# One stage in place of three: constants, first layer norm and the tables of q, k and v of a graph network on one NeuronCore

## The chip, the cores and the metric

The kernel runs on one core of one Trainium2 chip. The metric is device time in microseconds (us) of that core; lower is better. The core's engines are TensorE (PE in the rows; PEld is its weight load), VectorE (DVE), ScalarE (ACT), GpSimd (POOL) and SyncE (SP), which here issues DMAs. They run side by side and wait for each other through semaphores.

## The reference

The program is a two-layer graph network over N = 3125 nodes with 256 features and E = 50000 edges, sorted by destination. What the change touches is its very start: a layer norm of the nodes, three linear maps of it, and for each edge the product of its destination's key with its source's query.

```python
def _layernorm(x, axis=-1, eps=1e-05):
    m = jnp.mean(x, axis=axis, keepdims=True)
    v = jnp.var(x, axis=axis, keepdims=True)
    return (x - m) / jnp.sqrt(v + eps)
...
h = _layernorm(x)
q, k, v = h @ Wq.T + bq, h @ Wk.T + bk, h @ Wv.T + bv     # 3125 x 256 each
score[e, head] = sum over the head's 64 features of k[dst[e]] * q[src[e]]
```

These lines of the maps are told in short; in the program, softmax over each node's edges, sums of v, a global attention, experts, a graph convolution, a spline layer, an attention in the Poincare ball and a last layer of experts follow. All of them stay as they are.

## The kernel before, in words

Nodes lie in NT = 25 tiles of 128 rows (padded to 3200). Work is cut into stages; a stage has one instruction stream for each engine, and between two stages all engines meet at a barrier. A stage's `Chain` c(...) makes VectorE wait for each of its own instructions before the next.

The kernel begins with three stages, one after the other:

- `constants` (L266 on) loads the destinations of the edges and all of x, and builds what the later loops read: the identity `m.ident`, bf16 copies of the destinations (`m.lines`, `m.pick`, by GpSimd), and the list of steps. A step is a pair of 128-edge tiles and a window of 128 node slots. VectorE finds the ends of every run of edges (L338 to L353), TensorE sums counts (L384 to L386), VectorE compares 4992 step numbers with two columns (L363), TensorE turns that into words by 78 one-column products (L390), and the words go out to memory and come back as one row, `m.steps`.
- `layer_norm` (L143 on) does statistics of all 25 tiles (L158), seven small operations over all of them (L134 to L140), a square root on ScalarE (L188), a reciprocal, and 25 scalings (L169). Each tile is turned by two TensorE transposes (L180) and copied out by two ScalarE copies (L194) into `m.xT`.
- `node_tables` (L200 on) loads weights and biases, then for every tile makes three products of two 128x256 matmuls each (L234) in a ring of five PSUM banks; VectorE adds the bias of each (L246) and SP stores it to memory (L221): q and v side by side in `table_qv`, k in `table_k`.

Then `edge_scores` begins. Its SP stream first loads all of k back (L486) to the 25 first of 49 slots of `k`; ScalarE and VectorE copy it, shifted by half a tile, to the other 24 (L558, L802). Only then may TensorE's key products begin (L633). The loop goes by rounds of RING = 8 steps. For each step ScalarE copies two columns of source numbers (L519), GpSimd gathers 2 x 128 rows of `table_qv` by an indirect DMA each (L613) into one of eight buffers, TensorE spreads the edges' numbers (L625), VectorE makes a one-hot of them (L807), TensorE fetches the keys by it (L633), VectorE multiplies with the gathered q (L814) and reduces (L821), and SP stores the gathered v by edge (L503). GpSimd's gather of step s+8 waits for VectorE's multiplication of step s. Beside the steps TensorE and ScalarE do the work of a global attention: in the first five rounds (FIRST) a projection of two 128x320 matmuls every second step, in the next five (HIDE) a hidden layer and exponentials, then other pieces (SECOND, THIRD).

The order within each engine is the order in which the code is written; nothing schedules it.

Of the kernel before, what the change touches and what calls it, by code (L numbers as in the profile page):

```python
# [8 lines left out]
F32 = mybir.dt.float32  # L9
# [7 lines left out]
P = 128  # L17
# [108 lines left out]
def tiles_in(tt):  # L126

    return [tt * U + u for u in range(U)]


# [12 lines left out]
def layer_norm(nc, name, src, rows, cols, ident, banks, spread=None):  # L143


    with Stage(nc, name) as st:
# [3 lines left out]
        var_ready, std_ready, rows_ready = st.sem("var"), st.sem("std"), st.sem("rows")  # L150
        transposed, copied, own = st.sem("transposed"), st.sem("copied"), st.sem("own")
        with nc.Block() as block:
            @block.vector
            def _(dve):
                c = Chain(dve, own)
                with dve.Fori(0, TU) as tt:
                    for t in tiles_in(tt):
                        nc.vector.bn_stats(stats[:, bass.ds(t, 1), :], src[:, bass.ds(t, 1), :]).then_inc(own, 1)  # L158
                c.n = NT
                dve.wait_ge(own, NT)  # L160
                mean_and_variance(nc, c, stats, mv, rstd)
                if spread is not None:
                    c(nc.vector.tensor_copy(spread[:], mv[:, :, 1]))
                dve.sem_inc(var_ready, 1)
                dve.wait_ge(std_ready, 1)
                c(nc.vector.reciprocal(rstd[:], rstd[:]))
                with dve.Fori(0, TU) as tt:
                    for t in tiles_in(tt):
                        nc.vector.tensor_scalar(rows[:, bass.ds(t, 1), :], src[:, bass.ds(t, 1), :],  # L169
                                                mv[:, bass.ds(t, 1), 0], rstd[:, bass.ds(t, 1)],  # L170
                                                ALU.subtract, ALU.mult).then_inc(rows_ready, 1)

            @block.tensor
            def _(pe):
                for tt in range(TU):
                    for u in range(U):
                        pe.wait_ge(rows_ready, tt * U + u + 1)
# [17 lines left out]


def node_tables(nc, name, cols, weights, biases, tables, banks, spare):

    n = len(tables)
    with Stage(nc, name) as st:  # L200
        w = st.sb("w", [P, n, FT, F])
# [2679 lines left out]
```

## Time and profile before

| | us |
|---|---|
| three runs | 3152.86, 3153.89, 3155.55 (median 3153.89) |
| profiled execution, its own time | 3153.17 |
| its span, first to last instruction | 3151.5 |
| mean granted TensorE clock | 0.933 |

Over the whole span PE is busy 84%, DVE 63%, ACT 43%, POOL 34%. The shares are means over some dozen stages with different limits, and the change lies in the first 4% of the span and in what follows on it. So what has to be read is the timeline of the first 160 us and the loop behind it. All times in the rows count from the first instruction; they belong to the one profiled execution.

### The profile page before, as it was taken

What the parts mean: (1) busy time and instruction counts of PE and PEld (TensorE: products, weight loads), DVE (VectorE), ACT (ScalarE), POOL (GpSimd) and SP (SyncE); (2) the same over time, 40 slices, a digit from 0 to 9 for tenths busy, and PEclk for the clock granted to TensorE, in tenths of its full rate; (3) what the DMA queues carried; (4) which work ended last, traced back from release to release, by engine and by line L of the source; (5) the groups of instructions that cost most, each with busy time, mean ns of one, the idle gap of its engine ahead of it and who ended that gap; (6) DMA issues with size and microseconds to landing.
All of it is one profiled execution on the core that took longest, in us unless ns stands there. A gap on an engine that the chain in (4) does not pass through costs nothing. (4 is left out here: it accounts for less than half of the span.)

```text
span 3151.5 us, 54706 instructions
## 1 busy us (share of the span) xinstructions
PE 2657.6 (84%) x12020; PEld 2080.1 (66%) x12021; DVE 1989.4 (63%) x3891; ACT 1355.5 (43%) x2868; POOL 1074.7 (34%) x1184
## 2 busy tenths in 40 slices
PE   4677788737994899999997999999959996869798
PEld 3545555424552677777775888888848874647587
DVE  5386677877888444435214666666689986965411
ACT  1013332207882333333332444444459966855222
POOL 1276677742112000000003666666600006820043
PEclk9898899968997899999998999999979998989899
DMA  3698899956775000000004777777711114033253
GB/s 103 223 303 282 273 309 309 313 144 197 219 219 177 1 1 9 1 9 9 1 9 160 213 214 215 215 212 214 215 29 42 38 47 152 1 137 118 75 179 130
DMA packets 246940, 450.34 MB, mean 143 GB/s; under 512 B 29767, under 2 KB 142351, under 8 KB 245418
## 3 DMA queue, kind: packets, MB, share of 16 engines
q1 hardware_dynamic: 189868, 268.45, 27.2%
q0 software_dynamic: 56960, 180.47, 18.3%
q8 instruction: 62, 1.02, 0.1%
q14 instruction: 50, 0.41, 0.0%
HBM read 353.83 MB, written 95.96 MB: 143 GB/s over the span
## 5 line engine op out<-in xcount | busy, mean ns | idle before, releaser
L1826 PE MATMUL bank<-conv_w,conv_eT 128*128 128x256 f32 x2352 | 541.2, 380 | 4.2 <-DMA conv_eT<-in_edges 4.2
L1826 PEld LDWEIGHTS bank<-conv_w,conv_eT 128*128 128x128 f32 x2352 | 434.1, 190 | 56.2 <-DMA conv_eT<-in_edges 5.0
L1758 POOL DMA_INDIRECT conv_h<-table_h,conv_ix x392 | 389.0, 992 | 211.9 <-issue 113.1
L613 POOL DMA_INDIRECT x<-table_qv,scores_ix x300 | 283.8, 946 | 235.0 <-ACT scores_ix L519 157.0
L1523 ACT ACTIVATE area<-bank,nodes_bi,nodes_sc 128x320 f32<-128x320 f32 x320 | 197.5, 617 | 378.6 <-PE bank L1440 378.6
L1671 DVE SCALAR_TENSOR_TENSOR x<-bank,nodes_w,x 128x256 f32<-128x256 f32 x200 | 96.6, 484 | 324.4 <-PE bank L1449 324.3
L1782 DVE TENSOR_TENSOR conv_msg<-bank,conv_h 128x512 f32<-128x512 f32 x196 | 135.5, 692 | 193.8 <-PE bank L1826 193.8
L1290 PE MATMUL bank<-attend_pv,x 128*128 128x260 f32 x800 | 221.1, 404 | 30.4 <-POOL attend_pv L1221 26.4
L633 PE MATMUL bank<-sums,area 128*128 x800 | 233.0, 420 | 11.3 <-issue 6.3
L519 ACT ACTIVATE scores_ix<-src 128x2 int32 x200 | 40.5, 203 | 408.1 <-DVE area L814 327.7
L1290 PEld LDWEIGHTS bank<-attend_pv,x 128*128 128x128 f32 x800 | 137.2, 191 | 114.1 <-issue 66.2
L1725 ACT ACTIVATE conv_ix<-src 128x2 int32 x196 | 39.8, 203 | 366.6 <-DVE conv_msg L1782 344.2
L633 PEld LDWEIGHTS bank<-sums,area 128*128 128x128 f32 x800 | 154.3, 208 | 55.1 <-issue 31.1
L1181 ACT ACTIVATE x<-area,scores 128x128 f32 x400 | 157.3, 398 | 26.1 <-PE bank L1290 9.0
L1411 POOL MEMSET sums<- 128x1300 f32 x5 | 5.9, 1181 | 441.5 <-DVEq L1630 441.5
L1918 PE MATMUL bank<-xT,sums 128*128 128x256 f32 x700 | 155.2, 379 | 0.0
L625 PE MATMUL bank<-lines,pick 128*128 x200 | 58.4, 292 | 102.9 <-DVE area L807 70.4
L1918 PEld LDWEIGHTS bank<-xT,sums 128*128 128x128 f32 x700 | 133.0, 190 | 18.1
L814 DVE TENSOR_TENSOR area<-x,bank 128x512 f32<-128x512 f32 x150 | 103.0, 686 | 66.2 <-PE bank L633 56.2
L1238 DVE TENSOR_TENSOR attend_pv<-x,probs 128x512 f32<-128x512 f32 x198 | 135.9, 686 | 13.2 <-issue 13.2
L1839 PE MATMUL bank<-conv_coarse,conv_hot 128*128 128x256 f32 x392 | 137.9, 374 | 1.1 <-DVE conv_fine L1787 1.1
L821 DVE TENSOR_REDUCE scores_dot<-area 128x8 f32<-128x512 f32 x200 | 135.1, 675 | 0.1
(473 smaller groups left out, 5775.8 us busy)
## 6 DMA issues: line engine op xcount, KB each, us to landing
conv_eT<-in_edges SPq DMA_DIRECT2D x196, 384.0 KB
x<-edge_v SPq DMA_DIRECT2D x200, 256.0 KB, 3.0
edge_v<-x SPq DMA_DIRECT2D x150, 256.0 KB, 4.6
hidden_rows<-top_wide SPq DMA_DIRECT2D x25, 512.0 KB, 3.5
projected<-spline_hst SPq DMA_DIRECT2D x10, 960.0 KB, 4.4
ball_hT<-projected SPq DMA_DIRECT2D x5, 1920.0 KB, 19.1
top_wd<-in_top_wd SPq DMA_DIRECT2D x8, 1024.0 KB
table_qv<-sums SPq DMA_DIRECT2D x50, 128.0 KB, 1.7
```

Of the source, the lines that this page charges most:

```text
L613: nc.gpsimd.indirect_dma_start(out=qv(u)[:, g - u * G, :], out_offset=None, in_=m.d_qv, in_offset=bass.IndirectOffsetOnAxis(ap=ix[:, g:g + ...
L633: mm = nc.tensor.matmul(banks[u % UN][:, g * F:(g + 1) * F], hotT[:, u % UN, g * P:(g + 1) * P], k[:, bass.ds(t, 1), :].rearrange("p t f - ...
L821: nc.vector.tensor_reduce(dot[:, u % 2], qk[:, u % 2].rearrange("p (g h d) -> p g h d", g=G, h=HEADS), AX.X, ALU.add).then_inc(reduced, 1)
L1181: nc.scalar.activation(hot[:, u, g * P:(g + 1) * P], m.ids[:, bass.ds(t, 1)].rearrange("p t n -> p (t n)"), ACT.Abs, bias=minus[:, bass.ds ...
L1238: nc.vector.tensor_tensor(pv[:, u, :, 0:F].rearrange("p g (h d) -> p g h d", h=HEADS), v[:, u].rearrange("p g (h d) -> p g h d", h=HEADS), ...
L1290: mm = nc.tensor.matmul(banks[u][:, 0:WIDE], hot[:, u, g * P:(g + 1) * P], pv[:, u, g], start=g == 0, stop=g == G - 1)
L1523: nc.scalar.activation((h1, h2)[layer][:, o, hf * CW:(hf + 1) * CW], banks[n % HIDS][:, 0:CW], ACT.Relu, scale=sc[:, layer, e, o:o + 1], b ...
L1758: nc.gpsimd.indirect_dma_start(out=h[:, u, g, :], out_offset=None, in_=m.d_h, in_offset=bass.IndirectOffsetOnAxis(ap=ix[:, u * G + g:u * G ...
L1782: nc.vector.tensor_tensor(msg[:, u % 2], wide(u), h[:, u], ALU.mult).then_inc(messaged, 1)
L1826: mm = nc.tensor.matmul(banks[u][:, g * F:(g + 1) * F], eT[:, u, g, c], w[:, c], start=False, stop=c == EC - 1, skip_group_check=True)
L1839: nc.tensor.matmul(acc(u), hot[:, u, g], coarse[:, u, g], start=g == 0, stop=False)
L1918: mm = nc.tensor.matmul(out, spl[:, t % SETS, k, f * P:(f + 1) * P], ws[:, f, k], start=False, stop=f == FT - 1 and k == KS - 1)
```

## The change

The three stages become one, `front`. It loads x in five chunks of five tiles, and goes by chunks: `moments(n)` (statistics and the seven small operations on one chunk), `normal(n)` (reciprocal and five scalings), and for each tile two transposes, one copy, and the products of q, k and v. The step list's parts are put between the tiles, at tiles numbered by COUNT = 3 and LIST = 9. q and k use three PSUM banks, v two of its own: ScalarE writes v's bias into the bank ahead of the product (`seed`), the product is accumulated on it, and ScalarE copies it out (`keep_v`). VectorE adds the biases of q and k only; k's result goes straight to its slot in `keys`, which is `edge_scores`' `k`. q and v leave in one store. The table of k and its load are gone. The scratch for `number`, `lines_i`, `dst_i` and others moves to other buffers.

```diff
+def front(nc, a, m, banks):
...
+                def rows_of_x(n):
+                    sp.dma_start(m.x[:, tiles(n)], a["x"][n * U * P:(n + 1) * U * P].rearrange("(t p) f -> p t f", p=P)).then_inc(x_in[n], 16)
+                rows_of_x(0)
+                sp.dma_start(rows_i.rearrange("r g e -> r (g e)"), a["dst_scan"]).then_inc(pairs, 16)
+                for j, n in enumerate("qkv"):
+                    sp.dma_start(w[:, j], a[f"gnn_w{n}"]).then_inc(loaded, 16)
+                    sp.dma_start(b[:, j], a[f"gnn_b{n}"]).then_inc(loaded, 16)
+                rows_of_x(1)
                 for half in range(2):
                     sp.dma_start(lines_i[half * LINES:(half + 1) * LINES], a["dst_lines"]).then_inc(ends_loaded, 16)
+                for n in range(2, TU):
+                    rows_of_x(n)
...
+                for t in range(NT):
+                    sp.wait_ge(biased, 2 * t + 1)
+                    sp.wait_ge(kept_v, t + 1)
+                    sp.dma_start(m.d_qv[t * P:(t + 1) * P, :], qv[:, t % U]).then_inc(stored[t % U], 16)
...
+            @whole.tensor
+            def _(pe):
...
+                def turn(t):
+                    pe.wait_ge(rows_ready, t + 1)
+                    if t >= 2:
+                        pe.wait_ge(copied, t - 1)
+                    for f in range(FT):
+                        tr = nc.tensor.transpose(bank_x(t)[:, f * P:(f + 1) * P], m.rows[:, t, f * P:(f + 1) * P], m.ident[:])
+                    tr.then_inc(turned, 1)
+
+                def products(t):
+                    pe.wait_ge(copied, t + 1)
+                    for j in range(2):
+                        i = 2 * t + j
+                        if i >= 3:
+                            pe.wait_ge(biased, i - 2)
+                        for f in range(FT):
+                            mm = nc.tensor.matmul(bank(i), m.xT[:, f, t * P:(t + 1) * P], w[:, j, f], start=f == 0, stop=f == FT - 1)
+                        mm.then_inc(product, 1)
+                    pe.wait_ge(seeded, t + 1)
+                    for f in range(FT):
+                        mm = nc.tensor.matmul(bank_v(t), m.xT[:, f, t * P:(t + 1) * P], w[:, 2, f], start=False, stop=f == FT - 1,
+                                              skip_group_check=True)
+                    mm.then_inc(made_v, 1)
+                turn(0)
+                pe.wait_ge(loaded, 32 * KINDS)
+                for t in range(NT):
+                    if t + 1 < NT:
+                        turn(t + 1)
+                    products(t)
...
+            @whole.scalar
...
+                for t in range(NT):
+                    if t + 1 < NT:
+                        columns(t + 1)
+                    if t % U == 1 and t // U + 1 < TU:
+                        root(t // U + 1)
+                    keep_v(t)
+                    if t + 2 < NT:
+                        act.wait_ge(kept_v, t + 1)
+                        seed(t + 2)
...
+                moments(0)
                 dve.wait_ge(pairs, 16)
+                c(nc.vector.tensor_copy(rows_f, rows_i))
+                normal(0)
+                c(nc.vector.tensor_reduce(ends[:, 0], rows_f, AX.X, ALU.min))
...
+                dve.sem_inc(counted, 1)
...
+                for t in range(NT):
+                    n = t // U
+                    if t % U == 0 and n + 1 < TU:
+                        moments(n + 1)
+                    bias(t)
+                    if t % U == 2 and n + 1 < TU:
+                        normal(n + 1)
+                    if t == COUNT:
+                        first_steps()
+                    if t == COUNT + 1:
+                        compare(seen[:, 0:1], early)
+                    if t == COUNT + 3:
+                        compare(begin[:], late)
+                    if t == COUNT + 2:
+                        rounds()
...
 def edge_scores(nc, a, m, banks):
...
-                sp.dma_start(k[:, 0:NT], m.d_k.rearrange("(t p) f -> p t f", p=P)).then_inc(k_loaded, 16)
...
-                act.wait_ge(k_loaded, 16)
                 nc.scalar.activation(k[0:P // 2, NT:SLOTS], k[0:P // 2, 1:NT], ACT.Copy).then_inc(k_spread, 1)
```

Of the order, first TensorE at its start. In the program before, everything of the step list stands ahead of a barrier, then the transposes, then, behind another barrier, the products (`const_`, `norm_` and `qkv_` are the three stages' names):

```order
L384 MATMUL bank<-const_sums,const_before 99x1 [waits const_tables,const_made]
L385 MATMUL bank<-const_sums,const_next_to 99x1
L386 MATMUL bank<-const_one,const_sums 1x1
L390 MATMUL bank<-const_change,rows 128x1 [waits const_tables]
L390 MATMUL bank<-const_change,rows 128x1 x77
L287 UNCONDITIONAL_BRANCH
L173 UNCONDITIONAL_BRANCH [waits barrier_Pool_Activation_PE_DVE_SP_release]
L180 MATMUL bank<-ident,rows 128x128 [waits norm0_copied,norm0_rows]
```

In the changed one this is TensorE from the end of tile 2 to the transposes of tile 5 (`front_` is the stage; L290 are q and k, L294 is v):

```order
L305 MATMUL bank<-front_sums,front_before 99x1 [waits front_counted]
L306 MATMUL bank<-front_sums,front_next_to 99x1
L307 MATMUL bank<-front_one,front_sums 1x1
L280 MATMUL bank<-ident,rows 128x128 [waits front_copied,front_rows_ready]
L280 MATMUL bank<-ident,rows 128x128
L290 MATMUL bank<-front_w,xT 128x256 [waits front_biased,front_copied]
L290 MATMUL bank<-front_w,xT 128x256
L290 MATMUL bank<-front_w,xT 128x256 [waits front_biased]
L290 MATMUL bank<-front_w,xT 128x256
L294 MATMUL bank<-front_w,xT 128x256 [waits front_seeded]
L294 MATMUL bank<-front_w,xT 128x256
L280 MATMUL bank<-ident,rows 128x128 [waits front_copied,front_rows_ready]
```

The transposes and the products of a tile now alternate, and each q or k product waits for a bias addition of VectorE, three products back. The second place is VectorE around the first comparison. Before:

```order
L359 TENSOR_TENSOR const_begin<-const_seen,const_count 99x1 [waits const_own]
L360 TENSOR_TENSOR const_change<-const_slot,const_seen 99x1 [waits const_own]
L363 TENSOR_SCALAR rows<-sums,const_seen 99x4992 [waits const_made,const_own]
L363 TENSOR_SCALAR rows<-sums,const_begin 99x4992 [waits const_own]
L366 CAST dst<-const_dst_i 128x396 [waits const_own,const_edges]
```

Now, from the additions of tile 4 to the first addition of tile 5:

```order
L373 TENSOR_TENSOR front_qv<-bank,front_b 128x256 [waits front_product,front_own]
L375 TENSOR_TENSOR sums<-bank,front_b 128x256 [waits front_product]
L407 TENSOR_SCALAR area<-area,front_seen 99x4992 [waits front_numbered]
L357 BN_STATS front_stats<-x 128x6 [waits front_x_in2]
L357 BN_STATS front_stats<-x 128x6 x4
L129 TENSOR_TENSOR front_mean_var<-front_stats 128x5 [waits front_own]
L130 TENSOR_TENSOR front_rstd<-front_stats 128x5 [waits front_own]
L131 TENSOR_SCALAR front_mean_var<-front_mean_var 128x5 [waits front_own]
...
L135 TENSOR_SCALAR front_mean_var<-front_mean_var 128x5 [waits front_own]
L373 TENSOR_TENSOR front_qv<-bank,front_b 128x256 [waits front_own,front_stored0,front_product]
```

The comparison and a chunk's moments stand one behind the other between two pairs of additions for which TensorE waits.

## Rows read from the trace of the kernel before

**Rows 1.** Stages of the start: length, busy time of each engine, granted clock, DMA.

```profile
...
0.00:27.00 27.00, 3.16 (x84) 3.00 (x85) 18.27 (x35) 0.02 (x1) 11.64 (x20) 1.00 0.55 167
27.00:51.00 24.00, 8.89 (x50) 6.72 (x50) 18.66 (x59) 10.63 (x52) 0.00 (x0) 1.00 0.00 1
...
57.00:125.00 68.00, 66.96 (x300) 58.31 (x300) 31.83 (x75) 0.00 (x0) 0.00 (x0) 0.97 0.41 139
...
```

**Rows 2.** Timeline of the first 15 us: start, length, engine, line, operation, wait.

```profile
...
2.27 4.47 POOL L316 IOTA sums<- 99x4992 f32 x1
...
3.69 3.35 DVE L338 CAST const_rows_f<-const_rows_i 99x512 f32<-99x512 int32 x1 [3.57 <-DMA const_rows_i<-in_dst_scan]
...
8.92 0.99 DVE L343 TENSOR_SCALAR const_tile_i<-const_ends_i 99x2 int32<-99x2 int32 x1
...
9.97 2.36 POOL L329 TENSOR_TENSOR lines<-xT,lines 64x1152 bf16<-64x1152 f32 x1
10.14 2.21 DVE L345 CAST const_tile<-const_tile_i 99x2 f32<-99x2 int32 x1
...
13.86 0.16 DVE L353 SCALAR_TENSOR_TENSOR const_sums<-const_slot,const_count 99x1 f32<-99x1 f32 x1
...
```

**Rows 3.** DMA issues up to 140 us: count, size, median us to landing.

```profile
...
x<-in_x SPq DMA_DIRECT2D x1, 3200.0 KB, 14.2
...
```

**Rows 4.** Groups of instructions, 0 to 50 us: count, busy us, mean ns, idle.

```profile
...
L180 PE MATMUL bank<-ident,rows 128*128 128x128 f32 x50 | 8.9, 324 | 16.9 <-DVE rows L169 16.9
...
L158 DVE BATCH_NORM_STATS2 norm_stats<-x x25 | 8.4, 413 | 4.7 <-PEq L287 4.3 <-issue 0.3
L169 DVE TENSOR_SCALAR rows<-x,norm_mean_var,norm_rstd x25 | 8.4, 407 | 0.4 <-DVE norm_rstd L166 0.4
...
L363 DVE TENSOR_SCALAR rows<-sums,const_seen 99x4992 bf16<-99x4992 f32 x1 | 2.8, 2819 | 0.0
...
L390 PE MATMUL bank<-const_change,rows 99*128 99x1 bf16 x78 | 2.2, 165 | 6.5 <-DVEq L364 6.5
...
```

**Rows 5.** Groups of instructions, 51 to 125 us.

```profile
...
L234 PE MATMUL bank<-qkv_w,xT 128*128 128x256 f32 x300 | 67.0, 387 | 7.5 <-DMA qkv_b<-in_gnn_bv 7.5
...
L246 DVE TENSOR_TENSOR sums<-bank,qkv_b 128x256 f32<-128x256 f32 x75 | 31.8, 424 | 44.0 <-PE bank L234 44.0
```

**Rows 6.** Timeline of TensorE, 55 to 64 us.

```profile
...
57.14 7.17 PE L234 MATMUL bank<-qkv_w,xT 128*128 128x256 f32 x23 [7.46 <-DMA qkv_b<-in_gnn_bv]
```

**Rows 7.** Timeline from 124 us on: the end of the tables, the start of edge_scores.

```profile
...
124.14 0.42 DVE L246 TENSOR_TENSOR sums<-bank,qkv_b 128x256 f32<-128x256 f32 x1 [0.44 <-PE bank L234]
...
128.62 0.41 SPq L486 DMA_DIRECT2D sums<-table_k  x1
...
130.28 1.16 POOL L613 DMA_INDIRECT x<-table_qv,scores_ix  x1 [117.48 <-ACT scores_ix L519]
...
147.50 5.32 ACT L558 ACTIVATE sums<-sums 64x6144 f32<-64x6144 f32 x1 [14.90 <-DMA sums<-table_k]
147.50 3.39 DVE L802 COPY sums<-sums 64x6144 f32<-64x6144 f32 x1 [15.78 <-DMA sums<-table_k]
148.02 3.69 POOL L613 DMA_INDIRECT area<-table_qv,scores_ix  x1 [0.31 <-issue]
...
155.59 0.69 DVE L814 TENSOR_TENSOR area<-x,bank 128x512 f32<-128x512 f32 x1 [3.79 <-PE bank L633]
...
157.52 0.94 POOL L613 DMA_INDIRECT x<-table_qv,scores_ix  x1 [4.57 <-ACT scores_ix L519]
...
```

**Rows 8.** Group of ScalarE's copy out of PSUM, 125 to 175 us.

```profile
...
L567 ACT ACTIVATE rows<-bank 128x320 f32 x4 | 1.7, 437 | 0.4 <-PE bank L640 0.4
...
```

**Rows 9.** VectorE's timeline at the end of edge_scores' first five rounds.

```profile
...
246.87 0.69 DVE L814 TENSOR_TENSOR area<-area,bank 128x512 f32<-128x512 f32 x1
...
```

**Rows 10.** The gathers' line, 125 to 250 us: time to landing.

```profile
...
DMA to landing us min/median/max: 4.4/5.3/8.2
```

**Rows 11.** The gathers' line alone: POOL busy and count in a stretch.

```profile
...
175.00:250.00 75.00, 56.71 (x60) 1.00 0.97 314
...
```

More of the change, by code:

```diff
@@ new lines, in front @@
+        x_in = [st.sem(f"x_in{n}") for n in range(TU)]
+        filled, made, numbered, halved, named = (st.sem(x) for x in ("filled", "made", "numbered", "halved", "named"))
+        own, counted, added, begun, listed, worded, steps_kept = (
+            st.sem(x) for x in ("own", "counted", "added", "begun", "listed", "worded", "steps_kept"))
+        var_ready, std_ready, rows_ready, turned, copied = (
+            st.sem(x) for x in ("var_ready", "std_ready", "rows_ready", "turned", "copied"))
@@ new lines, in front, with tiles, bank, bank_v @@
+        opened, seeded, product, biased, made_v, kept_v = (
+            st.sem(x) for x in ("opened", "seeded", "product", "biased", "made_v", "kept_v"))
+        stored = [st.sem(f"stored{u}") for u in range(U)]
+        STORE_WORDS, COUNT, LIST = 17, 3, 9
+        def tiles(n):
+            return slice(n * U, (n + 1) * U)
+        def bank(i):
+            return banks[i % 3][:, 0:F]
+        def bank_v(t):
+            return banks[3 + t % 2][:, 0:F]
+        def bank_x(t):
+            return banks[5 + t % 2][:, 0:F]
@@ L359, in _ @@
-                c(nc.vector.tensor_tensor(begin[:], seen[:, 0:1], count[:, 0:1], ALU.add))
-                c(nc.vector.tensor_tensor(change[:, 0:1], slot[:, 0:1], seen[:, 1:2], ALU.subtract))
-                dve.wait_ge(made, 5)
-                for k, first in enumerate((seen[:, 0:1], begin[:])):
-                    c(nc.vector.tensor_scalar(begun[:, k], number, first, None, ALU.is_ge))
-                dve.sem_inc(tables, 1)
-                dve.wait_ge(edges, 16)
-                c(nc.vector.tensor_copy(m.dst[:], dst_i[:]))
@@ new lines, in compare, with rounds @@
+                def compare(first, to):
+                    dve.wait_ge(numbered, 1)
+                    nc.vector.tensor_scalar(to, number, first, None, ALU.is_ge).then_inc(begun, 1)
+                def rounds():
+                    for k, many in enumerate((UN, RING)):
+                        for j in range(2):
+                            c(nc.vector.tensor_scalar(m.rounds[:, 2 * k + j:2 * k + j + 1], banks[7][0:1, TOTAL_AT:TOTAL_AT + 1],
+                                                      float(many - 1 - j * many), float((FEWEST[many] - j) * many), ALU.add, ALU.max))
+                        c(nc.vector.tensor_scalar(m.rounds[:, 2 * k:2 * k + 2], m.rounds[:, 2 * k:2 * k + 2], many.bit_length() - 1, None, ALU.arith_shift_right))
@@ L395, in step_at @@
+                c(nc.vector.tensor_copy(m.twice[:], mv[:, :, 1]))
 def step_at(eng, m, s):
```

296 lines of the change are left out of this document (125 added, 171 removed).

## The prediction

> **What bounds the kernel now.** I read the stretches of the start first, then the timeline inside them, then the first rounds of the loop behind, since a gain at the start is kept only if nothing there gives it back.
>
> The start falls into four pieces, and in each another engine works [rows 1]. To 27 us VectorE is busy 18.3 us and TensorE 3.2. From 27 to 51 us VectorE works 18.7 us and TensorE 8.9. From 57 to 125 us TensorE is busy 67.0 of 68 us and VectorE 31.8. So TensorE's products are the longest piece, and some 57 us in which TensorE hardly works lie ahead of them. The products take 67.0 us for 300 records [rows 5]; the first 23 ran in 7.17 us [rows 6], at half clock in part. Twelve records make a tile. The other 277 take 59.8 us, 0.216 us each, 2.59 us a tile.
>
> Behind it, edge_scores begins at 128.62. Its k load holds VectorE's and ScalarE's copies until 147.50, the first score comes at 155.59, and GpSimd, which had begun to gather at 130.28, stands idle 4.57 us before 157.52 because all eight buffers are full [rows 7]. The k load is thus waited for, but what ends the first rounds is a second question: GpSimd issues 60 gathers in 75 us, one per 1.25 us and without a gap [rows 11], and a step needs two: 2.50 us. The fortieth score is at 246.87 [rows 9], so (246.87 - 155.59) / 39 = 2.34 us a step: TensorE and VectorE go faster than the gathers and eat up their lead. At that score some of it is left: the step's second gather was issued at 157.52 + 1.25 + 31 x 2.5 = 236.3, and with the median of 5.3 us to landing [rows 10] it was there at 241.6.
>
> **The change, part by part.** Times from here are laid out on the new program's own clock.
>
> *First chunk.* x in one piece landed 14.2 us after its issue [rows 3]; a fifth of it is 2.8 us, and the smallest load, 198 KB, took 2.8 us from 0.85 to 3.69 as well [rows 2]. I take 4.9 us for chunk 0, between 3.7 and 6. Statistics are 8.4 / 25 = 0.336 us a tile [rows 4], 1.7 a chunk. A small dependent operation costs about 0.19 us: twelve of them, L343 to L353, took 5.1 us, less the two that stood for GpSimd (0.8 and 2.0 over their own length) [rows 2]. Seven are 1.4 us, so moments(n) costs 3.1. The first tensor_scalar of moments(0) meets GpSimd's IOTA, 4.47 us, which held up L338 from 3.69 to its end at about 7 before [rows 2]; it now starts one 0.6 us memset later. moments(0) ends near 8.4, the root and the cast near 9, normal(0) (0.3 + 5 x 0.336 = 2.0) at 11.
>
> *Counting, and the second moments, ahead of the first addition.* Two reductions 1.4, fourteen small operations 2.7, and GpSimd's three copies of the lines, which now land after x0, the weights and x1 and so fall again into this chain: the two waits seen before (2.8 us) up to three (4.2). That is 19 us, 17.8 without the third wait. moments(1) stands next: 22.1. Only then bias(0). TensorE has begun by about 11, has made q, k, v of tile 0 and q of tile 1, and stops for a bank until 22.5.
>
> *From there on.* k and v of tile 1: 1.7. Twenty-three tiles at 2.59 for the products plus two transposes. These took 8.9 / 50 = 0.18 each [rows 4], paced by VectorE, which bounds them from above at 0.36 a tile; from below, half the columns of one product record, 0.108 each, 0.22 a tile. I take 0.30: 23 x 2.89 = 66.5. The 78 products of the list: 2.2 [rows 4]. After a pause of some 5 us the clock is low as at 57 us: 7.17 - 23 x 0.216 = 2.2 lost [rows 6]. ScalarE is no bound: three passes over 256 columns a tile, each no more than the 0.44 of a 128x320 one [rows 8], 1.3 of 2.9 us; they hide behind the products, and at over 2.9 would be the pace. VectorE needs 0.85 a tile for two additions [rows 5], and with moments, normals and comparisons some 48 of 75 us.
>
> *The ring of three banks.* From the end of q(t) TensorE has k, v, the next transposes and the next q before it, 2.9 us, until it needs q(t)'s bank back; VectorE is free 1.5 us ahead of q(t)'s end and needs 0.5 for the addition. So work of up to 3.9 us put ahead of an addition costs nothing. One moments(n) (3.1) or comparison (2.8 [rows 4]) fits. At tile 4 to 5 they stand together: 5.9, a stall of 2.1; the second comparison and normal(2) follow before VectorE has caught up: 0.7 more. Taken: 2.8. Bounds: 0, and 24 if nothing hid (three more moments 9.3, four normals 8, comparisons and small ones 9, less 2.8).
>
> So TensorE ends at 22.5 + 1.7 + 66.5 + 2.2 + 2.2 + 2.8 = 97.9. Before, from the last addition's release at 124.14 to edge_scores' first instruction at 128.62 it took 4.5 us [rows 7]: copy, store, landing, barrier. The same again gives 102.4 instead of 128.62: 26.2 us gained. The stores, one of 256 KB a tile instead of three of 128, are in the shadow of the products as before.
>
> *edge_scores.* Counted from its start. Before, the copies began at 18.9 and the first score stood at 27.0. Now ScalarE does its eight source copies (to 4.0) and then copies for 5.3 [rows 7]; the first score comes 14.8 earlier, at 12.2. GpSimd begins at 1.7 as before and is held up once by VectorE's 3.39 us copy, as its 3.69 us gather shows [rows 7]; that merely comes earlier. Without the 4.3 us that the full ring cost (4.57 less the usual 0.3), the second gather of step 8 starts at 157.52 + 1.25 - 4.27 - 128.62 = 25.9 and that of step 39 at 25.9 + 31 x 2.5 = 103.4; it lands at 108.7. The score of step 39 was at 118.3, and 14.8 earlier would be 103.5. The gathers now end last: 118.3 - 108.7 = 9.6 us gained, between 6.7 and 10.5 by the extremes of landing, 8.2 and 4.4 [rows 10]. Behind it comes other work per round, in which the ring was full again before, so I carry the 9.6 to the end.
>
> **Sum.** 26.2 + 9.6 = 35.8 from the profiled execution's 3153.17 is 3117.4; the median of the runs is 0.7 above that execution, so 3118.
>
> **The rivals.**
> (a) *The gathers swallow the k load's share.* If GpSimd's chain sets the pace not only of these rounds but of all of edge_scores, only its 4.3 us of idleness are gained: 26.2 + 4.3, 3123. For it: 1.25 us without a gap [rows 11]. Against: the fortieth score before did not wait for them.
> (b) *VectorE as the bound of the new stage.* If the three banks hide nothing, 24 us instead of 2.8: 3139. For it: VectorE alone is busy 37 us in the two early stages [rows 1], and all of this now goes between additions. Against: the slack of 3.9 us.
> (c) *Slower: TensorE stays at half clock in front.* It now mixes transposes and waits for three other engines into what was a closed run of products. At half clock a tile costs 2.59 us more, 23 tiles 60 us: 3178. It turns a gain into a loss from 35.8 / 2.59, 14 tiles, on. Against it: the transposes alone stood at granted clock 1.00 between 27 and 51 us [rows 1], the products at 0.97 with their cold start; gaps above 5 us are not foreseen after the first.
> The Trainium skill speaks for (c): TensorE: Matmul & The Clock Gate, section Part 4: PE-mode transpose, says that a transpose does not count as busy for the clock. By that rule the two transposes of each tile would be idle time, a tenth of it; the trace before, with 1.00 over a stretch of transposes alone, does not show it, though that stretch began in quiet and is weak evidence.
> (d) *Front starts earlier or its order stalls less:* no lock waits and no stall, 4.2 + 2.8 less: 3111. This and the like lie in the forecast's own range.
>
> **How the numbers follow.** The forecast's case, 3108 to 3128: 0.72. (a) alone lies in it; with a start worse by 5 to 8 us it leads to 3132: 0.08. (b) or half of it, 3130 to 3142: 0.12. (c) 0.02. Better than 3108, with the full 14.8 us of k and a start without locks (3118 - 5.2 - 7): 0.06. The range 3106 to 3132 leaves out about 2 in 10. A difference under 0.2% (6 us) can't be told from none in this kernel. Faster by more than that: all but (c) and an unknown of the same size, 0.96; within 0.01; slower 0.03.
>
> **What would show it.** Right: TensorE pauses from about 17 to 22 us and once near tiles 4 to 6; the products' pace between is 2.8 to 3.0 us a tile; edge_scores' first instruction at 98 to 107 us; the first score 12 us later; in the first five rounds VectorE's multiplication waits for the gathers' landing, not for TensorE, and GpSimd has no idle time but 0.3 us a piece. Wrong: TensorE waiting for VectorE at every chunk (b), a granted clock under 0.9 in front (c), rounds of HIDE or later that are longer than before, or scores 40 and 200 whose distances from edge_scores' start have shrunk by other than some 10 us.

## The result, and the profile after

The changed kernel takes 3103.07 us, the median of 4 runs (3099.56 to 3106.83), against 3154.47 us for the kernel before on the same chip. The ratio on record is 0.9844, with a 95% interval from 0.9828 to 0.9861 (the two medians by themselves would give 0.9837). Two later batches on other chips came to 0.9848 and 0.9858. The forecast was 3118 us, with a range from 3106 to 3132: the sign was right, the gain was larger than forecast, and the median lies 2.9 us below the range. The three ratios average 0.9850, a gain of 47.3 us; by that figure the time would be near 3107 us, just inside the range, so a miss of the range by this little is in part the scatter of one batch. The gain itself is a third larger than the 35.8 us forecast, and that is no scatter. The profiled execution has a span of 3097.9 us and a time of its own of 3099.56 us.

The stretches of the new start, one line each (length, busy time of each engine, granted clock, DMA share, GB/s), in place of those of [rows 1]:

```profile
0.00:22.00 22.00, 9.48 (x26) 6.62 (x27) 15.07 (x49) 4.25 (x11) 11.57 (x20) 1.00 0.91 257
24.00:94.00 70.00, 67.82 (x404) 58.93 (x403) 41.67 (x124) 24.50 (x70) 0.00 (x0) 0.98 0.23 85
```

One stretch of TensorE's work is left where there were two of VectorE's ahead of one of TensorE's. From 24 to 94 us TensorE is busy 67.8 of 70 us. The timeline of the changed kernel shows how it gets there (start, length, engine, line, operation, and the wait in brackets):

```profile
2.55 4.47 POOL L251 IOTA area<- 99x4992 f32 x1
5.48 1.73 DVE L357 BATCH_NORM_STATS2 front_stats<-x 128x6 f32<-128x256 f32 x5 [5.36 <-DMA x<-in_x]
7.25 0.17 DVE L129 TENSOR_TENSOR front_mean_var<-front_stats 128x5 f32<-128x5 f32 x1
...
9.47 1.71 DVE L367 TENSOR_SCALAR rows<-x,front_mean_var,front_rstd 128x256 f32<-128x256 f32 x5
...
11.10 3.78 PE L290 MATMUL bank<-front_w,xT 128*128 128x256 f32 x8
...
15.25 1.73 DVE L357 BATCH_NORM_STATS2 front_stats<-x 128x6 f32<-128x256 f32 x5
15.77 1.14 POOL L259 CAST sums<-sums 128x1152 f32<-128x1152 int32 x1 [8.50 <-DMA sums<-in_dst_lines]
16.97 1.15 POOL L261 CAST lines<-sums 128x1152 bf16<-128x1152 f32 x1
17.02 1.12 DVE L129 TENSOR_TENSOR front_mean_var<-front_stats 128x5 f32<-128x5 f32 x1
18.17 0.17 DVE L130 TENSOR_TENSOR front_rstd<-front_stats 128x5 f32<-128x5 f32 x1
18.20 2.37 POOL L263 TENSOR_TENSOR lines<-sums,lines 64x1152 bf16<-64x1152 f32 x1
18.37 2.22 DVE L131 TENSOR_SCALAR front_mean_var<-front_mean_var 128x5 f32<-128x5 f32 x1
...
21.61 0.42 DVE L373 TENSOR_TENSOR front_qv<-bank,front_b 128x256 f32<-128x256 f32 x1
22.09 1.50 PE L290 MATMUL bank<-front_w,xT 128*128 128x256 f32 x4 [4.70 <-DVE front_qv L373]
...
40.82 1.13 PE L290 MATMUL bank<-front_w,xT 128*128 128x256 f32 x4 [2.18 <-DVE front_qv L373]
...
64.31 0.38 PE L280 MATMUL bank<-ident,rows 128*128 128x128 f32 x2
64.53 1.89 PE L290 MATMUL bank<-front_w,xT 128*128 128x256 f32 x8
...
67.13 0.38 PE L280 MATMUL bank<-ident,rows 128*128 128x128 f32 x2
...
94.15 1.03 PE L294 MATMUL bank<-front_w,xT 128*128 128x256 f32 x4
```

TensorE pauses twice: for 4.70 us, until VectorE has made the first addition of tile 0 and a bank is free, and for 2.18 us at tile 5. Two operations of five columns that take 0.17 us elsewhere take 1.12 and 2.22 us and end 0.02 us after GpSimd's operations of 16.97 and 18.20 do; these are the waits that [rows 2] showed in the counting, now in moments(1). A tile takes 67.13 - 64.31 = 2.82 us.

The start of edge_scores, in place of [rows 7], and VectorE's multiplication of the fortieth step, in place of [rows 9]:

```profile
99.20 0.34 SPq L542 DMA_DIRECT2D vec<-in_mix_wk  x1
...
100.78 1.16 POOL L667 DMA_INDIRECT x<-table_qv,scores_ix  x1 [79.75 <-ACT scores_ix L574]
...
102.25 3.54 POOL L667 DMA_INDIRECT x<-table_qv,scores_ix  x1 [0.30 <-ACT scores_ix L574]
102.31 3.36 DVE L855 COPY sums<-sums 64x6144 f32<-64x6144 f32 x1
...
102.76 5.31 ACT L612 ACTIVATE sums<-sums 64x6144 f32<-64x6144 f32 x1
...
110.83 0.69 DVE L867 TENSOR_TENSOR area<-x,bank 128x512 f32<-128x512 f32 x1 [4.26 <-PE bank L687]
...
208.01 0.69 DVE L867 TENSOR_TENSOR area<-area,bank 128x512 f32<-128x512 f32 x1 [0.57 <-DMA area<-table_qv,scores_ix]
```

edge_scores starts at 99.20 instead of 128.62, the first score comes 11.6 us after that instead of 27.0, and the fortieth at 108.8 instead of 118.3. What the fortieth waits for is the gather's landing, as forecast; nine of the forty multiplications waited for a landing, 4.6 us in all, and GpSimd was never idle for more than 0.3 us between gathers.

In the profiled executions the lead of the changed kernel is 29.4 us at the start of edge_scores and 38.9 us at the fortieth score, 3.1 more than the 35.8 of the sum. But it ends at 3151.5 - 3097.9 = 53.6 us. The other 14.7 us arise where the code is the same, so the experiments went after them above all. This table gives, from the trace of every kernel that ran, edge_scores' start; the first and fortieth score counted from it; the length of scores 41 to 81 (the HIDE rounds); the length of the attention sums (the stage behind edge_scores that sums v over each node's edges), from their first instruction to the start of TensorE's last product; what follows that; and the span. All in us.

| kernel | start | first | fortieth | HIDE | attention | behind | span |
|---|---|---|---|---|---|---|---|
| before | 128.6 | 27.0 | 118.2 | 122.1 | 248.7 | 2183.3 | 3151.5 |
| before, again | 129.6 | 27.2 | 118.9 | 121.4 | 248.8 | 2187.0 | 3159.0 |
| after | 99.2 | 11.6 | 108.8 | 117.3 | 243.6 | 2179.5 | 3097.9 |
| after, again (two) | 98.7, 99.9 | 11.6, 11.6 | 108.1, 109.2 | 117.5, 119.3 | 244.5, 244.0 | 2177.6, 2181.7 | 3098.1, 3104.4 |
| k through memory | 98.6 | 27.4 | 118.3 | 119.4 | 243.7 | 2181.1 | 3115.3 |
| after, paused | 106.3 | 11.7 | 108.2 | 117.7 | 243.7 | 2179.2 | 3108.5 |
| before, 75 memsets (two) | 131.9, 131.5 | 27.5, 27.0 | 118.2, 117.9 | 119.4, 119.8 | 244.0, 244.4 | 2181.1, 2178.8 | 3145.0, 3144.0 |
| before, 75 and 61 | 132.2 | 27.3 | 119.6 | 121.4 | 244.0 | 2178.3 | 3145.1 |
| after, reordered | 90.0 | 11.6 | 108.5 | 119.4 | 244.0 | 2181.4 | 3094.2 |
| after, comparisons later | 98.0 | 11.6 | 108.8 | 120.2 | 244.3 | 2178.6 | 3101.4 |
| after, v's bias on VectorE | 102.5 | 11.9 | 108.2 | 120.7 | 248.8 | 2179.0 | 3107.9 |
| after, 25 memsets | 99.3 | 11.6 | 108.1 | 119.2 | 249.3 | 2179.5 | 3106.0 |

### The profile page after: what moved, and what is told of

It is laid out like the page before. It is cut to its first block and busy times, and to the rows that moved or that the text cites. A ratio compares the mean times of both kernels' runs of the same rounds, so it can differ in the third digit from the quotient of the medians.

```text
span 3097.9 us, 54276 instructions
## 1 busy us (share of the span) xinstructions
PE 2648.6 (85%) x12024; PEld 2070.9 (67%) x12025; DVE 1979.6 (64%) x3898; ACT 1370.0 (44%) x2897; POOL 1067.3 (34%) x1184
## 3 DMA queue, kind: packets, MB, share of 16 engines
q1 hardware_dynamic: 179516, 261.89, 27.2%
```

## The experiments

**1. Both kernels again.** Nothing is edited.

> The changed kernel once more, nothing altered. Theory 1 (the forecast's two terms are caused by the change, the rest of the gain is not): edge_scores again starts at 99.2 us and its fortieth score comes 108.8 us later, both within 0.5 us, while the rounds behind, the attention sums and the node layers differ from the first profiled execution by some us in sum, in either direction; total 3098 to 3107. Theory 2 (everything that is gained behind the fortieth score is caused by the change as well): those stages too repeat to within 1 us in sum, total 3099 to 3101.

> The kernel before once more. Theory 1: edge_scores at 128.6 and the fortieth score 118.3 us later, within 0.5; later stages differ from the first execution by some us in sum, in either direction. Theory 2: all stages repeat within 1 us.

Measured: 3104.59 us (median of 5, ratio 0.9848, 0.983 to 0.9866), and one run of the kernel before at 3160.75, beside 3152.7 for its median in that batch. The start of edge_scores and the fortieth score repeat within 1 us, not within the 0.5 expected (128.6 and 129.6, 118.2 and 118.9; 99.2 and 98.7, 108.8 and 108.1). The attention sums too repeat within 1 us in both kernels, 248.7 and 248.8 against 243.6 and 244.5, so the 5 us between the kernels are no chance. What lies behind them differs by 3.7 us between two executions of the kernel before. So neither theory holds whole: the attention sums repeat, the rest behind the fortieth score does not.

**2. Keys through memory again.** The new front, but k goes to the table of k and is read back before the copies:

```diff
+                    sp.dma_start(m.d_k[t * P:(t + 1) * P, :], keys[:, t]).then_inc(k_kept, 16)
...
+                sp.dma_start(k[:, 0:NT], m.d_k.rearrange("(t p) f -> p t f", p=P)).then_inc(k_loaded, 16)
```

> The changed kernel with k also stored to memory, one 128 KB store a tile, and loaded back at the start of edge_scores, where the copies wait for it as before the change: only the front part of the gain is left. Theory 1: edge_scores starts at 99 to 101 us, the fortieth score 118 us after that, 9.5 us later than in the changed kernel, and the total is 9 to 11 us above it. Rival (the gathers set the pace of all of edge_scores): 4 to 5 us above it. Rival (the whole advance of the first score counts): 15 us above it.

Measured: 3114.82 us (3112.04 to 3117.04), ratio 0.9878 (0.9862 to 0.9893), 10.2 us above the changed kernel of the same batch. The first score is back at 27.4 us and the fortieth at 118.3. So the 9.6 us that the sum gave to this part are right at the fortieth score, where 9.5 are seen, and they do not get lost behind it: the two hundredth and last score comes 541.5 us after edge_scores' start here, against 525.1, 526.7 and 528.2 in the three executions of the changed kernel (the rounds between add scatter of their own). The timed 10.2 us alone would say less, since runs of the changed kernel in this batch spread over 14 us. The attention sums stay at 243.7 us: neither k's way nor its load is their cause.

**3. A pause ahead of everything.** A stage with one memset on GpSimd stands before the new front.

```diff
+        with Stage(nc, "pause") as st:
...
+                        nc.gpsimd.memset(m.rows[:], 0.0).then_inc(done, 1)
```

> The changed kernel behind a stage that holds one GpSimd memset of 25 tiles, about 6 to 7 us with its barrier; everything else is as it was, only later. If later stages depend on nothing but their own work, the total is above the changed kernel's by just the pause, 6 to 7 us. If they depend on where they stand in time (the clock's, or the phase of two engines), the total differs from that by several us and the profile names the stage.

Measured: 3113.44 us (3110.22 to 3117.33), 8.9 above the changed kernel for the 7.6 us by which edge_scores started later than in that kernel's profiled execution of the same batch (6 to 7 were expected of the pause). Time at the front reaches the end one to one within the scatter, and the attention sums stay at 243.7 us although they begin 10 us later.

**4. The place of the code.** An instruction's start is in the trace for register and branch instructions too. This is the time in ns from the start of the branch at the end of a loop's pass to the start of the next instruction on that engine; it is the same in nearly every pass of a loop:

```
                        before   again   after   again   75 memsets   75 and 61   25 on after   v on VectorE
VectorE, HIDE rounds       300     300     281     281          281         281           281            281
VectorE, attention sums    267     267     191     191          191         191           280            280
VectorE, convolution       267     267     272     272          176         176           280            280
ScalarE, HIDE rounds       155     155     155     155          155         237           155            155
ScalarE, convolution       155     155     226     226          155         226           226            155
```

The loops are word for word the same; what differs is how many instructions stand ahead of them. So memsets of one element, whose result nobody reads, were put ahead of them in the kernel before, and then in the changed one.

```diff
+                for n in range(75):
+                    nc.vector.memset(pad[:, n:n + 1], 0.0)
                 c(nc.vector.scalar_tensor_tensor(packed[:], banks[2][:, 0:COLS], 1.0, place[:], ALU.mult, ALU.add))
```

> The kernel before, with 75 one-element memsets more on VectorE in its constants stage (work that nobody waits for), so that all VectorE code behind stands 75 instructions later, about as in the changed kernel. Nothing else differs. Theory (the place of the code of a loop sets how long the jump back takes): in the attention sums VectorE's next instruction starts 267 ns after its loop's branch in both runs of the kernel before and 191 ns in all four with the new front; here it should come at 191 or at another fixed value than 267, and with it the length of the attention sums should leave 248.7 us (towards 243.7, if VectorE alone decides). Rival (something that the new front leaves in memory or in time): 267 ns and 248.7 us stay as they are.

> The kernel before, with the 75 memsets on VectorE and 61 one-element copies on ScalarE in its constants stage, so that the code of both engines stands about as late as in the changed kernel. Theory (place of code): attention sums 243.5 to 245 us instead of 248.7, of a round of eight steps 9.34 us instead of 9.55; ScalarE's branches in edge_scores' second loop and in the edge convolution take other times than 155, 237 and 155 ns. For the HIDE rounds (steps 40 to 80 of edge_scores, 122.1 and 121.4 us before, 117.3 to 117.7 after) the theory says nothing certain: if they fall to 117.5 too, it was the code's place there as well; if they stay at 122, it was the lead of the gathers. Rival (what the front leaves behind): 248.7 and 9.55 stay.

> The kernel before with the 75 memsets on VectorE, now timed. Theory (place of VectorE's code, worth 4.7 us in the attention sums of its look, less what the memsets cost at the front, where edge_scores started at 132.4 us instead of 128.6 to 129.6): the two nearly cancel in the total, ratio 0.998 to 1.000, while the attention sums stay at 244.0 and the HIDE rounds lie between 119 and 122 us. Rival (the look's 3146.7 us showed a gain of the whole kernel of 4.5 us): ratio 0.9985 or below. If the HIDE rounds come at 121 to 122 again, the 119.4 of the look was chance of the clock; at 119.4 again, it belongs to the program.

Measured: 191 ns in all three, and 244.0, 244.0 and 244.4 us of attention sums. ScalarE's 61 copies changed its own jumps but not this stage: VectorE alone decides it. Timed, the kernel with 75 memsets takes 3145.65 us against 3151.3, ratio 0.9985 (0.9974 to 0.9996), although edge_scores starts some 2.6 us later in it (131.9, 131.5 and 132.2 us in the three padded executions, counted from the load of k, against 128.6 and 129.6; the memsets stand ahead of the packing of the words). This ratio lies within the range of the theory and at the edge of the rival's, so it does not decide between them; it shows a small gain of the whole kernel. The question on the HIDE rounds stayed open as well: 119.8 us. Then the same in the other direction:

```diff
+                for n in range(25):
+                    nc.vector.memset(pad[:, n:n + 1], 0.0)
                 moments(0)
```

> The changed kernel, with 25 one-element memsets on VectorE ahead of its first moments, where it waits for x until 5.4 us. VectorE's code behind then stands where it stands in the kernel with v's bias on VectorE, in which the jump of the attention sums took 280 ns and the stage 248.8 us. Theory (place of VectorE's code): 280 ns instead of 191, attention sums 248.8 instead of 243.7 us, edge_scores' start within 0.5 us of 99, in all 4 to 6 us slower than the changed kernel by the runs on one chip. Rival (the 248.8 us there came with the other load of ScalarE and VectorE): 191 ns and 243.7 us stay, within 2 us of the changed kernel.

> The changed kernel again, beside the one with 25 memsets, as its control on the same chip: ratio 0.984 to 0.985. Its HIDE rounds (steps 40 to 80 of edge_scores) took 117.3 and 117.5 us at a granted clock of 0.86 and 0.83. If their length hangs on the clock and the clock on chance, a third execution may show 118 to 122 at 0.75 to 0.80; if it belongs to the program, 117 to 118 again.

Measured: 280 ns, attention sums of 249.3 us, edge_scores' start at 99.3, and 3109.29 us against 3104.76 on the same chip, ratios 0.9872 (0.985 to 0.9893) and 0.9858 (0.9837 to 0.988): 4.5 us more. The intervals of the two ratios overlap, so what is clear of noise is the stage in the trace and not the total. The direction and the size fit. VectorE's rows at the jump (start, length, line, the wait before) show the mechanism; first the kernel before:

```profile
903.08 0.42 DVE L1248 TENSOR_TENSOR sums<-sums,bank 128x260 f32 x1
904.05 0.69 DVE L1238 TENSOR_TENSOR attend_pv<-x,probs 128x512 f32<-128x512 f32 x1 [0.55 <-issue]
```

then the changed one:

```profile
854.23 0.43 DVE L1301 TENSOR_TENSOR sums<-sums,bank 128x260 f32 x1
855.11 0.69 DVE L1291 TENSOR_TENSOR attend_pv<-x,probs 128x512 f32<-128x512 f32 x1 [0.46 <-issue]
```

the one before with 75 memsets:

```profile
900.57 0.69 DVE L1241 TENSOR_TENSOR attend_pv<-x,probs 128x512 f32<-128x512 f32 x1 [0.46 <-issue]
```

and the changed one with 25:

```profile
852.72 0.69 DVE L1294 TENSOR_TENSOR attend_pv<-x,probs 128x512 f32<-128x512 f32 x1 [0.56 <-issue]
```

"issue" before VectorE's first multiplication of a pass holds the jump. The clock is no rival in this stage; over the attention sums of the kernel before, the changed one and the changed one with 25 memsets, the rows are

```profile
719.40:968.10 248.70, 220.67 (x799) 137.24 (x800) 214.96 (x402) 209.96 (x602) 48.49 (x201) 0.97 0.73 215
674.80:918.40 243.60, 219.42 (x800) 136.96 (x800) 214.87 (x402) 206.13 (x602) 47.16 (x201) 0.97 0.75 220
677.20:926.50 249.30, 219.85 (x800) 137.16 (x800) 216.89 (x402) 207.58 (x602) 50.81 (x201) 0.97 0.73 215
```

with the same granted clock of 0.97 and TensorE busy for the same time within 1.3 us. Over 24 passes the jump's 0.08 us make 1.9 us. A pass takes 9.55 us in the kernel before and 9.34 in the changed one, so the rest of the 0.21 comes after: most steps take 1.08 us, and in the kernel before one more step of each pass takes 1.20. Why it takes longer there was not taken apart.

A jump that moves need not cost anything. VectorE's in the convolution went from 267 to 176 ns with the 75 memsets, 4.4 us over its 48 passes, and that stage lasted 630.1 and 630.6 us without them and 630.8, 630.4 and 630.7 with them. TensorE is busy 608.7 of the 630.1 us there and VectorE 416.0.

**5. TensorE's two pauses.** moments(1) and ScalarE's root of it are moved behind the second tile's additions, and the comparisons two tiles back, with the list:

```diff
-                    if t % U == 0 and n + 1 < TU:
+                    if t % U == 0 and 0 < n and n + 1 < TU:
                         moments(n + 1)
                     bias(t)
+                    if t == 1:
+                        moments(1)
...
-                    if t == COUNT + 1:
+                    if t == COUNT + 3:
                         compare(seen[:, 0:1], early)
...
```

> The changed kernel, with two moves in the new stage: VectorE's moments of the second chunk stand behind the bias of tile 1 (ScalarE's root of it likewise behind keep_v of tile 1), and the two comparisons of the step list stand at tiles 6 and 8 instead of 4 and 6, TensorE's list two tiles later. Theory (the first bias waits behind moments(1), whose small instructions GpSimd holds up, and tile 5 waits behind a comparison): TensorE's pauses of 4.7 us at the third tile and 2.2 us at tile 5 go, edge_scores starts 5 to 7 us earlier than 98.7 to 99.2, near 93, and all of it reaches the end: near 3097 to 3099 us. Rival A (tile 4 then waits for the second chunk's moments, which are as slow behind bias(1)): the pause moves to tile 4 and 0 to 2 us are won. Rival B (GpSimd's chain of table, gathers and node numbers is what edge_scores' start really hangs on): the start does not move.

> The changed kernel with only the second move of the reordered one: the two comparisons of the step list at tiles 6 and 8, TensorE's list two tiles later; moments(1) stays ahead of bias(0). Theory: TensorE's pause of 4.7 us before the third tile's products stays, the one of 2.2 us at tile 5 goes, edge_scores starts near 97 (99.2 less 2.2), and the rest of the 9.2 us that the reordered kernel won is moments(1)'s. Rival (the two pauses share a cause, the comparison is only late because the first bias was): the pause at tile 5 moves one or two tiles on, and the start stays at 99.

Measured: 3095.87 us (3092.43 to 3099.86), ratio 0.9825 (0.9812 to 0.9839). It is the fastest kernel of the study. edge_scores starts at 90.0, 9.2 us earlier, which is more than the two pauses (6.9) and more than the 5 to 7 expected; in the time some 8 us arrive (ratio 0.9825 beside the changed kernel's 0.9850). TensorE's clock shows most of the rest. In the changed kernel the windows behind the first pause and on from it have

```profile
22.00:24.00 2.00, 1.91 (x6) 1.59 (x7) 1.07 (x4) 0.00 (x0) 0.00 (x0) 0.68 0.36 129
24.00:42.00 18.00, 15.82 (x77) 13.34 (x76) 12.15 (x39) 5.61 (x16) 0.00 (x0) 0.94 0.18 68
```

and the reordered one has, over the whole of it,

```profile
16.00:87.00 71.00, 69.61 (x414) 60.12 (x412) 46.12 (x142) 25.23 (x74) 3.85 (x4) 1.00 0.31 113
```

A granted clock of 0.68 for 2 us and 0.94 for 18 against 1.00 is some 1.7 us of the missing 2.3. With only the comparisons moved (one run, 3103.13 us) the pause at tile 5 is gone as expected, but the first pause is 5.55 us instead of 4.70, and edge_scores starts at 98.0 instead of the 97 expected. That start is worth only 1.2 us, but behind the longer first pause the clock also stayed low for longer, as this row of that kernel shows:

```profile
24.00:42.00 18.00, 18.00 (x85) 15.31 (x84) 11.21 (x41) 5.82 (x17) 0.00 (x0) 0.89 0.20 74
```

So most of the 9.2 us are moments(1)'s, and how much exactly one run does not tell.

**6. v's bias on VectorE.** The product starts afresh, and VectorE adds v's bias as it does k's.

```diff
+                    dve.wait_ge(made_v, t + 1)
+                    nc.vector.tensor_tensor(qv[:, t % U, F:2 * F], bank_v(t), b[:, 2], ALU.add).then_inc(kept_v, 1)
```

> The changed kernel, with v's bias back on VectorE: its third product starts afresh, ScalarE neither seeds nor copies v, VectorE adds 128x256 from PSUM per tile more. By the trace VectorE has 1.1 us of work per tile of 2.81 (q's and k's bias) besides moments, normal and the list, and one addition more of 0.36 us makes 1.5 to 1.6 per tile, on average below TensorE's pace: theory: tiles stay at 2.8 us, the front ends within 2 us of 99, total within 3 us of the changed kernel. Rival (ScalarE was given the bias because VectorE is full where moments, comparisons and additions meet): the stalls at tiles 2 and 5 and at each chunk grow by 0.4 to 1.5 us each, edge_scores starts 4 to 8 us later and the time is 3107 to 3111.

Measured: 3113.41 us (3109.61 to 3117.62), ratio 0.9885 (0.9869 to 0.99). edge_scores starts at 102.5, 3.3 us later: TensorE's pauses are 5.26, 3.05, 0.31 and 0.33 us instead of 4.70 and 2.18. The theory's "within 2 us of 99" failed by that, and the rival's 4 to 8 us and 3107 to 3111 us were missed a little on either side. Another 5 us of the loss have nothing to do with the bias: with 25 more additions on VectorE the jump of the attention sums took 280 ns and the stage 248.8 us, which is what the 25 memsets of experiment 4 gave by themselves.

## Why the prediction missed

*First chunk.* Forecast: x lands at 4.9, moments(0) ends near 8.4, normal(0) at 11. Measured: 5.48, 8.6, 11.2. Right. (The working counts twelve small operations from L343 to L353; they are eleven, so one costs 0.20 instead of 0.19 us, 0.2 us in all.)

*Counting, second moments, first addition.* Forecast: TensorE goes on at 22.5; measured 22.09. The lock waits were laid in the counting (4.2 us) and fell in moments(1), 0.95 + 2.05 = 3.0 us over the usual 0.17, since the lines landed late. The sum was nearly right with the waits in another place.

*From there on.* 75.4 us were forecast to TensorE's end and 73.1 measured. The transposes were sized wrongly: the lower bound of 0.22 us a tile was the truth and 0.30 was taken (23 x 0.08 = 1.8). The stall at tile 4 to 5 was forecast at 2.1 and measured at 2.18; the further 0.7 did not come. The low clock behind the first pause cost 1.7 instead of 2.2; three small products of the counting, which the sum left out, took 0.5 (28.42 to 28.90). From TensorE's end to edge_scores 4.0 us instead of 4.5. Together the front gains 29.4 instead of 26.2 us.

*edge_scores.* First score 11.6 after the start (forecast 12.2), fortieth 108.8 (forecast 108.7), and 10.2 us in the total by experiment 2 (forecast 9.6). Here the row of the gathers' line in the changed kernel alone is the counterpart of [rows 11]:

```profile
125.00:200.00 75.00, 56.73 (x61) 0.95 0.97 314
```

Rival (a) is out: had the gathers paced all of edge_scores, only 4.3 us of it would have stayed, against the 10.2 in the time and 13 to 16 at the two hundredth score in experiment 2.

*The step that failed* is the sum's last: "so I carry the 9.6 to the end", and nothing else from there on. It took the stages behind as unchanged because their code is. The prediction had named the sign itself, scores 40 and 200 nearer to edge_scores' start "by other than some 10 us": the fortieth came nearer by 9.4, the two hundredth by 15.2 (540.3 to 525.1; 543.0 in the other execution of the kernel before, 526.7 and 528.2 in the changed one's). Inserted and removed instructions ahead of them moved VectorE's code, and the attention sums alone became 4.3 to 5.1 us shorter, which is shown in both directions. The front's 3.2 us are the smaller part of the miss. The closing account: the three ratios of the changed kernel average 0.9850, 47.3 us of 3152. The kernel before gains 0.0015 x 3151 = 4.7 us by its 75 memsets (1.3 to 8.2 by the interval) while it starts edge_scores about 2.6 us later for them, so the place of the code is worth some 7.3 us, 3.9 to 10.8. That leaves 40.0 us for the change itself, 36.5 to 43.4, against 35.8 + 3.2 = 39.0 by the sum with the front as measured. This is an estimate: it takes the two programs' code as equally placed, and outside the attention sums it is not (the jumps in the table).

*What stays open* is the part of those 7.3 us outside the attention sums. The HIDE rounds took 121.4 to 122.1 us in the kernel before, 119.4 to 121.4 with memsets and 117.3 to 120.7 behind the new front. Their windows, of the kernel before,

```profile
252.40:374.60 122.20, 88.57 (x324) 63.80 (x325) 77.81 (x171) 46.67 (x95) 78.46 (x83) 0.76 0.86 267
```

of the changed kernel,

```profile
213.60:330.90 117.30, 80.64 (x324) 56.80 (x325) 77.73 (x171) 46.67 (x95) 81.70 (x87) 0.86 0.93 292
```

and of a second execution of that,

```profile
215.00:334.30 119.30, 85.60 (x324) 61.30 (x325) 77.78 (x171) 46.72 (x95) 81.57 (x87) 0.80 0.91 287
```

show nearly the same counts of instructions on TensorE, VectorE and ScalarE and another granted clock: 0.76, 0.86, 0.80. TensorE's burst for the hidden products shows it in single rows of the changed kernel:

```profile
287.19 2.94 PE L720 MATMUL bank<-wg,scores_room 128*128 128x64 f32 x20 [1.78 <-ACT scores_room L594]
...
309.30 4.43 PE L720 MATMUL bank<-wg,scores_room 128*128 128x64 f32 x20 [1.75 <-ACT scores_room L594]
```

So the HIDE rounds are mostly shorter where the clock is higher, and it varies from one execution of a program to the next. In the kernel with the comparisons moved 120.2 us stand beside a clock of 0.85, so it is not all. Whether the code's place moves the clock's chances was not settled. Behind the attention sums 2 to 9 us separate the kernels, and executions of one kernel differ there by 4. Part of that goes with the clock too; the attention in the Poincare ball, in two executions of the changed kernel, is

```profile
2546.50:2737.70 191.20, 137.36 (x600) 105.96 (x600) 156.64 (x217) 137.07 (x214) 139.83 (x83) 0.92 0.17 63
2545.60:2742.00 196.40, 142.81 (x600) 109.65 (x600) 156.77 (x217) 137.08 (x214) 139.82 (x83) 0.89 0.17 62
```

with the same instructions and 5.2 us between them.

*The clock in front.* Rival (c) did not come: the granted clock was 0.98 from 24 to 94 us and 1.00 from 42 to 94, with two transposes in every tile. The Trainium skill's statement that a transpose doesn't count as busy in the same way (TensorE: Matmul & The Clock Gate, Part 4: PE-mode transpose) is neither borne out nor refuted by it, since the products fill nine tenths of each tile. The prediction's own evidence against (c), the 1.00 of [rows 1] between 27 and 51 us, was weaker than it looked: the trace of the kernel before has no record of the clock before 44.04 us, and a row counts time without a record as 1.00. The last section shows what such a row can hide.

*Rival (b)*, VectorE as the bound, is out too: it waits for TensorE between additions, and even v's bias on top cost 3.3 us.

## What to carry to other kernels

In a sum that ends at a loop which the change does not touch, leave some room for the loop itself: count the instructions that the change adds or removes ahead of it on each engine, and where two kernels differ behind the change, compare first, engine by engine, the time from a loop's branch to its next instruction. Padding with one-element instructions whose result nobody reads can tell such a difference from a real one: here the first padded program already had the changed kernel's 191 ns and its attention sums. And a moved jump matters only where its engine is on the path, as the convolution shows. And where small operations stand ahead of what the bounding engine waits for, move the whole group behind the first such release: that, with the comparisons moved too, was worth 9.2 us at the start of edge_scores here, when each operation seemed to cost 0.2.

## What the runs showed of the hardware

The time from a loop's branch to the next instruction, 191, 267 or 280 ns on VectorE in the attention sums' loop, was the same in every execution of a program and changed with the number of instructions ahead. ScalarE's loops show it too (155 or 237 ns in the HIDE rounds, 155 or 226 in the convolution). With 24 passes and VectorE on the path it was worth 5 us of 249. The Trainium skill bears on it in Runtime: NRT & Kernel Launch, section Instruction fetch mechanics: instructions are fetched in blocks of 256, and a taken branch to a target outside the two blocks held makes the engine wait for a fetch. The runs agree that the place matters, but they show 0.08 us more or less rather than a transfer's length, and no run here shows where a block ends.

TensorE's first products behind a stay of hardly any work ran at half the later pace, eight in 3.78 us at 11.10 against 1.89 at 64.53, while the stretch's row in the changed kernel shows a granted clock of 1.00:

```profile
9.90:14.30 4.40, 4.32 (x12) 3.20 (x13) 4.06 (x15) 1.14 (x4) 0.00 (x0) 1.00 1.07 197
```

The trace's records of the clock begin only at 15.89 us, with the upper level; the 1.00 of this row stands for no record. The pace turns where the records begin: four products took 1.63 us at 14.67 and 1.03 at 16.36. In the reordered kernel, whose records begin at 13.83, the same eight took 3.31. So TensorE most likely ran at the lower level, 1.2 GHz, until then, and at the start of a program the rows' own durations have to be read instead of the granted clock.
